# Weights of seven experts split ahead of time by GpSimd, and their halves loaded from scratch memory

## The reference

```python
x = x + L0_ffn(L0_cond(x, itok_B_1_198, ...), ...)
x = x + L1_ffn(L1_cond(x, itok_B_0_7, ..., fside_8xS_0), ...)
# cond: w = weights[index[b]]; out = einsum('bct,bcd->bdt', x, w) (+ bias[b] in layer 1)
# layer 0 ffn: 8 experts of rank 8 (LoRA) on a shared 512 -> 2048 -> 512 with gelu, top 2
#   h = gelu(x W1' + b1 + 2 z1 B1), y = h W2' + b2 + 2 z2 B2, res += w_topk[k] * y
# layer 1 ffn: top 2 of 8 experts, hidden width 352, and a shared expert, hidden width 704
g = silu(einsum('td,edh->teh', x, w_gate)) * einsum('td,edh->teh', x, w_up)
routed = einsum('teh,ehd,te->td', g, w_down, comb)
shared = silu(x @ sw_gate) * (x @ sw_up) @ sw_down
out = routed + shared
```

## Time and profile before

| | |
|---|---|
| median of 3 runs | 1048.93 us |
| the profiled execution, own time | 1050.06 us |
| its span | 1048.2 us |
| TensorE busy | 1010.6 us (96%) |
| VectorE, ScalarE, GpSimd busy | 50%, 30%, 34% |
| mean granted TensorE clock | 0.993 |
| DMA over the span | 136.41 MB, 130 GB/s |

### The profile page before, as it was taken

One profiled execution on the slowest core, in us unless ns is written; L12 is line 12 of the kernel. 1 busy time (PEld: TensorE's weight loads), 2 busy tenths in 40 slices (PEclk: granted clock), 3 DMA queues, 4 the chain that ended last, 5 costly groups with the idle time before them and its releaser, 6 DMA issues.

```text
span 1048.2 us, 14852 instructions
## 1 busy us (share of the span) xinstructions
PE 1010.6 (96%) x4893; PEld 837.2 (80%) x4895; DVE 524.3 (50%) x886; ACT 314.4 (30%) x550; POOL 354.5 (34%) x351
## 2 busy tenths in 40 slices
PE   8899999999999999999999999999989999999993
PEld 5678887888888887888867777778778999999992
DVE  3788777455565455555566333665543314443000
ACT  3743332211121112111242010301144545454541
POOL 4123245410000000000042000022168889898873
PEclk9999999999999999999999999999999999999997
DMA  7387543443433434453444101005155665665433
GB/s 239 130 297 272 161 136 122 166 161 114 140 123 121 153 128 161 142 181 123 138 159 151 41 1 41 1 1 198 58 187 108 163 163 142 141 146 119 80 61 40
DMA packets 51322, 136.41 MB, mean 130 GB/s; under 512 B 8708, under 2 KB 10004, under 8 KB 50772
## 3 DMA queue, kind: packets, MB, share of 16 engines
q1 hardware_dynamic: 36660, 108.15, 30.1%
q0 software_dynamic: 12432, 25.71, 12.4%
q10 hardware_dynamic: 2192, 2.08, 0.7%
HBM read 96.85 MB, written 39.07 MB: 130 GB/s over the span
## 4 chain that ended last, share of the span: by engine, by line
PE 85%; DVE 4%; POOL 4%; DMA 2%; issue 1%; ACT 1%; ACTq 1%; PEldq 0%; POOLq 0%; PEld 0%; DVEq 0%
PE ps_y L1687 6%; PE ps_y L1689 6%; PE ps_y L1688 5%; PE ps_h L1645 5%; PE ps_h L1647 5%; PE ps_h L1646 5%; PE ps_u L1700 3%; PE ps_u L1699 3%; PE ps_h L1933 2%; PE ps_y L1933 2%; PE ps_y L1928 2%; PE ps_y L1929 2%; PE ps_y L1856 2%; PE ps_y L1857 2%; PE ps_h L1840 2%; PE ps_h L1841 2%
## 5 line engine op out<-in xcount | busy, mean ns | idle before, releaser
L1202 DVE TENSOR_TENSOR h<-h,wb 128x512 f32<-128x512 f32 x64 | 44.4, 693 | 162.6 <-ACT h L903 162.5
L897 ACT ACTIVATE h<-ps_h,bias 128x512 f32<-128x512 f32 x64 | 44.0, 689 | 235.1 <-PE ps_h L1654 235.1
L685 POOL DMA_DIRECT2D s_raw<-in_sgu x8 | 4.3, 544 | 299.9 <-DVE g_lo L1210 192.1
L1687 PE MATMUL ps_y<-w_hi,g_hi 128*128 (+1 forms) x256 | 102.2, 399 | 3.5 <-DVE g_lo L1210 3.5
L1689 PE MATMUL ps_y<-w_hi,g_lo 128*128 (+1 forms) x256 | 101.2, 395 | 0.0
L1688 PE MATMUL ps_y<-w_lo,g_hi 128*128 (+1 forms) x256 | 101.0, 395 | 0.0
L1645 PE MATMUL ps_h<-xt_hi,w_hl 128*128 128x512 f32 x256 | 100.0, 391 | 0.7 <-ACT lg_t L846 0.7
L1647 PE MATMUL ps_h<-xt_hi,w_hl 128*128 128x512 f32 x256 | 100.3, 392 | 0.0
L1646 PE MATMUL ps_h<-xt_lo,w_hl 128*128 128x512 f32 x256 | 100.2, 391 | 0.0
L1477 DVE CAST eg_hi<-e_raw 128x704 fp32r<-128x704 f32 x32 | 16.7, 581 | 138.0 <-PE ps_y L1958 125.3
L903 ACT ACTIVATE h<-ps_h,bias 128x512 f32<-128x512 f32 x64 | 43.9, 688 | 115.4 <-PE ps_h L1667 115.4
(11 more groups left out here) (319 smaller groups left out, 2455.5 us busy)
## 6 DMA issues: line engine op xcount, KB each, us to landing
w_hl<-w1s_d SPq DMA_DIRECT2D x49, 704.0 KB, 4.1
w1s_d<-w_hl SPq DMA_DIRECT2D x16, 704.0 KB, 5.9
e_raw<-in_wgu SPq DMA_DIRECT2D x8, 1408.0 KB, 7.1
w_raw<-in_w1b SPq DMA_DIRECT2D x16, 608.0 KB, 4.7
xres<-in_x SPq DMA_DIRECT2D x16, 256.0 KB, 4.5
acc<-x_d SPq DMA_DIRECT2D x4, 1024.0 KB, 7.6
xc_d<-xc SPq DMA_DIRECT2D x4, 1024.0 KB, 4.8
e_raw<-in_wdn SPq DMA_DIRECT2D x8, 512.0 KB, 8.4
```

Of the source, the lines that this page charges most:

```text
L1202: tt(h1[u][:], h1[u][:], wb[:, v, :], ALU.mult).then_inc(gch, 1)
L1687: mm(ps_y[:, j, :], g_hi[u][:, cols], sl(w2_hi), start=first, **kw)
```

## The change

The raw weights of experts 1 to 7 are laid out by the host as `we1`, (7, 128, 4608): per partition gate and up (2816 numbers), down (1536), and padding. GpSimd splits them in layer 0, from the end of the first super tile on, in 42 units of 128 x 768 (six for an expert): it loads a unit, casts it to `pre_hi`, stores that to scratch memory `e_d`, subtracts in place and stores the low half. The raw units go through two buffers for the first units and then three, two of which lie in `u1t`; the high halves through two. Unit k is loaded at the earliest when step 16 + (k - 2) is over. VectorE's first shared split, GpSimd's own and SyncE's first load of halves wait until all units are stored, since their destinations share memory with the units' buffers or they read them. Expert 0 stays as it was.

In the routed stage SyncE loads the four finished pieces of an expert straight into the buffers that TensorE reads (`load_halves`, 11264 and 6144 bytes a partition) and then counts the expert as done. VectorE makes xg_lo, rg and rgt_lo, reading PSUM itself, so that ScalarE's copies xg_f, ru and rgt_f are gone; xg_hi and xg_lo have two buffers. TensorE turns x of tile t+2 before up of tile t+1, and x of tile 0 within the last shared super tile. Tiles 0 and 1 are gathered without waiting for the last shared gate. GpSimd keeps the gathers and scatters; tile t is scattered right after its own gather step. A matrix of layer 1's conditioning and its bias column are one load, two for each w1 split, between the splits.

```diff
+    UNITS, UW = 6, we1.shape[2] // 6
+    AHEAD = UNITS * (E - 1)
+    IN_TWO = 8
+    raw_of = [k % 2 if k < IN_TWO else (k - IN_TWO) % 3 for k in range(AHEAD)]
+    raw_used = [raw_of[:k].count(raw_of[k]) for k in range(AHEAD)]
+    e_d = scr("e_d", (E - 1, 2, P, UNITS * UW))
...
+        pre_hi = [sb_ahead(f"pre_hi{u}", [P, UW], F32R)[:] for u in range(2)]
+        pre_raw = [sb_ahead("pre_raw0", [P, UW])[:], u1t[:, 0:UW], u1t[:, UW:2 * UW]]
...
-            for s in range(NS):
+            def load_halves(e):
+                b, gu = e % 2, DC * 2 * H1
+                for k, (eg, ed) in enumerate(((eg_hi, ed_hi), (eg_lo, ed_lo))):
+                    sp.dma_start(eg[:, b].rearrange("p c n -> p (c n)").bitcast(F32),
+                                 e_d[e - 1, k, :, 0:gu]).then_inc(half_in, 16)
+                    sp.dma_start(ed[:, b].rearrange("p c n -> p (c n)").bitcast(F32),
+                                 e_d[e - 1, k, :, gu:gu + HC * D]).then_inc(half_in, 16)
+            for s in range(NS - 1):
                 store_acc(s)
+            for u in range(2):
+                sp.wait_ge(pre_hi_st[u], 16 * (AHEAD // 2))
+            for u in range(3):
+                sp.wait_ge(pre_lo_st[u], 16 * raw_of.count(u))
+            sp.wait_ge(gu_done, NS * SH)
+            load_halves(1)
+            store_acc(NS - 1)
             for e in range(1, E):
-                load_expert(e)
+                if e >= 2:
+                    tiles = sp.value_load(last_tile[0:1, e:e + 1], min_val=0, max_val=SLOT_TILES)
+                    sp.wait_ge(ry_done, 1 + tiles)
+                    load_halves(e)
+                sp.wait_ge(half_in, 64 * e)
+                sp.wait_ge(e_done, e)
+                sp.sem_inc(e_done, 1)
...
+            def load_unit(k):
+                u = raw_of[k]
+                pool.wait_ge(d_done, 2 + FT + max(k - 2, 0))
+                if u == 2 and not raw_used[k]:
+                    pool.wait_ge(z_ok, 6)
+                if raw_used[k]:
+                    pool.wait_ge(pre_lo_st[u], 16 * raw_used[k])
+                at = k % UNITS * UW
+                pool.dma_start(pre_raw[u], we1[k // UNITS, :, at:at + UW]).then_inc(pre_in[u], 16)
+            def high_unit(k):
+                u = k % 2
+                pool.wait_ge(pre_in[raw_of[k]], 16 * (raw_used[k] + 1))
+                if k >= 2:
+                    pool.wait_ge(pre_hi_st[u], 16 * (k // 2))
+                nc.gpsimd.tensor_copy(pre_hi[u], pre_raw[raw_of[k]]).then_inc(pre_hi_done, 1)
+                pool.wait_ge(pre_hi_done, k + 1)
+                at = k % UNITS * UW
+                pool.dma_start(e_d[k // UNITS, 0, :, at:at + UW], pre_hi[u].bitcast(F32)).then_inc(pre_hi_st[u], 16)
+            def low_unit(k):
+                raw = pre_raw[raw_of[k]]
+                nc.gpsimd.tensor_tensor(raw.bitcast(F32R), raw, pre_hi[k % 2].bitcast(F32), ALU.subtract)\
+                    .then_inc(pre_lo_done, 1)
+                pool.wait_ge(pre_lo_done, k + 1)
+                at = k % UNITS * UW
+                pool.dma_start(e_d[k // UNITS, 1, :, at:at + UW], raw).then_inc(pre_lo_st[raw_of[k]], 16)
+            def units(ks):
+                for k in ks:
+                    high_unit(k)
+                    if k <= IN_TWO:
+                        load_unit(k + 1)
+                    if IN_TWO <= k < AHEAD - 2:
+                        load_unit(k + 2)
+                    low_unit(k)
+            shared_at = (NS - 2) * FT + 2
+            load_unit(0)
+            units(range(shared_at))
...
+            units(range(shared_at, AHEAD))
...
             for t in range(SLOT_TILES):
-                g_low(t)
-                if t + 1 < SLOT_TILES:
-                    products(t + 1)
-                if t + 2 < SLOT_TILES:
-                    x_low(t + 2)
                 if t + 5 < SLOT_TILES:
                     gather(t + 5)
-                if t:
-                    scatter_add(t - 1)
-            scatter_add(SLOT_TILES - 1)
+                scatter_add(t)
...
-            def x_high(t, first=False):
+            def x_high(t, u):
                 act.wait_ge(xgt_done, t + 1)
-                nc.scalar.copy(xg_hi[:].rearrange("p c n -> p (c n)"), ps_u[:, 0, :]).then_inc(xg_hi_done, 1)
-                if not first:
-                    act.wait_ge(xg_lo_done, t)
-                nc.scalar.copy(xg_f[:], ps_u[:, 0, :]).then_inc(xg_f_done, 1)
+                nc.scalar.copy(xg_hi[u][:].rearrange("p c n -> p (c n)"), ps_u[:, 0, :]).then_inc(xg_hi_done, 1)
...
+                else:
+                    for u in range(2):
+                        dve.wait_ge(pre_hi_st[u], 16 * (AHEAD // 2))
+                    for u in range(3):
+                        dve.wait_ge(pre_lo_st[u], 16 * raw_of.count(u))
...
-            for e in range(1, E):
-                dve.wait_ge(e_in, 48 * (e + 1))
-                if e >= 2:
-                    tiles = dve.value_load(last_tile[0:1, e:e + 1], min_val=0, max_val=SLOT_TILES)
-                    dve.wait_ge(ry_done, 1 + tiles)
-                for k in range(4):
-                    split_expert(e, e % 2, k)
+            def x_low(t, u):
+                dve.wait_ge(xg_hi_done, t + 1)
+                tt(xg_lo[u][:].rearrange("p c n -> p (c n)"), ps_u[:, 0, :],
+                   xg_hi[u][:].rearrange("p c n -> p (c n)").bitcast(F32), ALU.subtract).then_inc(xg_lo_done, 1)
+            def products(t, u, first=False):
+                dve.wait_ge(rs_done, t + 1)
+                dve.wait_ge(rup_done, t + 1)
+                if not first:
+                    dve.wait_ge(rgt_done, t)
+                tt(rg[:, 0:H1], rs[:], ps_y[:, u, 0:H1], ALU.mult).then_inc(rg_done, 1)
+            def g_low(t):
+                dve.wait_ge(rgt_hi_done, t + 1)
+                tt(rgt_lo[:].rearrange("p c n -> p (c n)"), ps_u[:, 1, 0:HC * P],
+                   rgt_hi[:].rearrange("p c n -> p (c n)").bitcast(F32), ALU.subtract).then_inc(rgt_lo_done, 1)
+            def slot_tile(t, u, nxt=True, nxt2=True):
+                g_low(t)
+                if nxt2:
+                    x_low(t + 2, u)
+                if nxt:
+                    products(t + 1, 1 - u)
...
+                    if (s, j) == (NS - 1, 0):
+                        turn_x(0, 0, 16, first=True)
...
                     gate_or_up(t + 1, 1 - u, after, 0)
                 turn_g(t)
+                if nxt2:
+                    turn_x(t + 2, x_buf, n)
                 if nxt:
                     gate_or_up(t + 1, 1 - u, after, 1)
```

More of the change, by code:

```diff
@@ L339, in adaln_ffn @@
         out_st = sem("out_st")
+        pre_in = [sem(f"pre_in{u}") for u in range(3)]
+        pre_hi_done = sem("pre_hi_done")
+        pre_lo_done = sem("pre_lo_done")
+        pre_hi_st = [sem(f"pre_hi_st{u}") for u in range(2)]
+        pre_lo_st = [sem(f"pre_lo_st{u}") for u in range(3)]
+        half_in = sem("half_in")
         e_in = sem("e_in")
@@ L442, in load_block, with load_matrix @@
                           cond0[bass.ds(b * SEQ, SEQ), :]).then_inc(landed, 16)
[L444 to L453, removed]
+        def load_matrix(eng, j, h):
+            at = j * 2 + h
+            b = eng.value_load(it_row[1][0:1, at:at + 1], min_val=0, max_val=cond1.shape[0] // SEQ - 1)
+            eng.dma_start(cw1[h * SEQ:(h + 1) * SEQ, j, :], cond1[bass.ds(b * SEQ, SEQ), :]).then_inc(cw1_in[h], 16)
         @block.sync
@@ L1036, in copies @@
                     silu(t + 1, 1 - u)
-                g_high(t, first=stored is None and n == 0)
-                if nxt:
-                    up(t + 1, 1 - u)
+                g_high(t)
                 if nxt2:
-                    x_high(t + 2)
+                    x_high(t + 2, u)
                 weigh(t, n, stored)
-            x_high(0, first=True)
+            x_high(0, 0)
             silu(0, 0, first=True)
-            up(0, 0)
-            x_high(1)
+            x_high(1, 1)
             act.wait_ge(sy_done, NS * TPS)
@@ L1544, in _ @@
                             split_expert(0, 0, k)
[L1547 to L1553 removed]
+            def x_low(t, u):
[18 more added lines that the diff above has]
+                    products(t + 1, 1 - u)
+            x_low(0, 0)
+            x_low(1, 1)
+            products(0, 0, first=True)
+            for t in range(2):
+                slot_tile(t, t)
+            with dve.Fori(1, (SLOT_TILES - 2) // 2) as m:
+                for u in range(2):
+                    slot_tile(m * 2 + u, u)
+            for t in range((SLOT_TILES - 2) // 2 * 2, SLOT_TILES):
+                slot_tile(t, t % 2, t + 1 < SLOT_TILES, t + 2 < SLOT_TILES)
         @block.tensor
@@ L1869, in slot_sums, with turn_x @@
                 last.then_inc(oh_mm, 1)
+            def turn_x(t, u, n, first=False):
+                pe.wait_ge(xg_in[u], n)
+                if not first:
+                    pe.wait_ge(xg_lo_done, t)
+                for c in range(DC):
```

(10 more changed lines are left out.)

99 lines of the change are left out of this document (39 added, 60 removed).

## The result

The changed kernel takes 1076.82 us (median of 4 runs, 1074.62 to 1080.04), the kernel before beside it 1049.45 us (4 runs): a ratio of 1.0259, 95% interval 1.0237 to 1.0281. It is slower by 27 us; 1039.0 was forecast, and the range ended at 1053.

What follows compares the result with a forecast made beforehand. TensorE's in-order queue was taken as the bound. Terms of -5.3, -5.7, -4.4 and +5.5 us sum to -9.9, from 1048.93 to 1039.0 us; range 1031.5 to 1053 us.

Steps and rivals of the forecast that it cites:

- Layer 0, VectorE: GpSimd's unit arithmetic holds up VectorE's chain before g_lo in layer 0: 0 to 0.5 us a unit, taken as +5.5 us.
- the second rival: In layer 0, GpSimd's copy and subtraction make TensorE wait for g_lo: 0.6 us a unit, 25 us, 1058 us; chance 0.10.
- The opening: At the start of the routed stage, reordered turns and earlier gathers remove TensorE waits: -5.3 us.
- The rest of the routed stage: Over the later routed tiles, 5.7 of the 6.2 us that TensorE loses to waits are taken back.
- The end: After the last weighings, scatters no longer queue behind the next tile's GpSimd operations: -4.4 us.
- The fourth rival: In the routed stage, double bytes make experts late and scatters lag, so only the opening is earned: 1049 us; chance 0.06.
- The transfers in layer 0: 1.15 MB more per step in layer 0 still lets w_hl's reload land in time: no cost, 0.8 us from one.
- GpSimd in time: GpSimd finishes all 42 units before VectorE's first shared split, at a period of 7.7 us: no cost.
- the third rival: GpSimd's unit period in layer 0 exceeds 8.0 us, so VectorE's first shared split waits: 1044 to 1056 us; chance 0.12.

Runs made afterwards that it cites:

- the gap and the chain: Changed kernel, complete, with each unit's rounding and subtraction started after VectorE's last operation of a step: 1051.01 us; started at ScalarE's second gelu instead: 1064.13 us.
- the first experiment: Changed kernel without GpSimd's arithmetic on the units, except two roundings; all loads, stores and landing waits stay: 1037.48 us, ratio 0.9872.

## Why the prediction was wrong

**The step that failed** is "Layer 0, VectorE", put at 0.13 us for each of 42 units, 5.5 us in all, with an upper bound of 0.5. It was 1.0 us, 42.1 in all, which is what the second rival says, and more than its 0.6. Two things in it were wrong.

The phase. I wrote that at 7.7 against 7.4 us it drifts and about every third unit falls on the chain. 35 of 42 did. A drift needs two clocks, and there weren't two: the subtractions are 8.54 us apart (42 from 173.97 to 523.95) and the steps in that time 8.57. It is not the hold that ties them together. With the rounding alone the steps are back at 7.39 us and the units with them (the roundings start at 385.86, 393.24 and 400.67), and with the moves alone the units are 7.38 us apart. In all three kernels most loads of a unit wait for the landing of a low half (27 of 42 in the changed kernel, 37 with the moves alone), so the units follow a cycle of transfers that runs beside SyncE's one reload a step; whether that ties them is not shown. Nor is why they keep to the chain when the subtraction is there (31 of 42 start in it or within 0.3 us before it) and to the time behind it when only the rounding is. What the gap and the chain show is that the place decides, at the same work. With the phase held in the chain on purpose a unit cost 0.74 us.

The length. I counted one hold against the spare 1.5 us, of "up to its own length". In the bad phase the subtraction and the next unit's rounding follow each other within 0.9 us (330.47 to 331.33), each catches another operation of the same chain, and their holds add: 2.95 us. The bound of 0.5 a unit, about 2.1 less 1.5, left out the second hold and was no bound; the lengths themselves were put too high (1.86 and 0.84 us measured, up to 2.1 each forecast). The evidence I leaned on, that 16 splits before cost only 3 waits, had one long GpSimd subtraction a step, issued at one place.

**What was right.** The opening: 5.3 forecast, 5.9 measured from the end of the shared stage; the forecast had the 0.5 us of tile 0's turn in it, so 5.4 by its own counting. The rest of the routed stage: 5.7 against 7.8, since all 6.2 us of waits went and the cadence fell from 6.745 to 6.70 us, 1.6 us in 36 tiles: the two tiles that I had read as free of waits took 6.69 and 6.79, and now every tile takes 6.70. The end: 4.4 against 3.3; from tile 37's weighing to the end (1058.85; 1028.37 before) it is 16.5 instead of 19.8 us, less than forecast because the scatters did lag: that of tile 37 starts 1.8 us behind its weighing, not 0.3. The chain that ended last is nearly all one scatter behind the other from 953 us on, and the first two of these are the long ones:

```profile
958.90 9.93 DMA out_x<-yt,slot_tok
...
993.12 9.57 DMA out_x<-yt,slot_tok
...
1061.33 4.49 DMA out_x<-yt,slot_tok
```

Their 9.9 and 9.6 us, twice the usual 4.5 to 5, fall into loads of an expert's halves. SyncE issues six such loads in the routed stage (at 838, 865, 905, 932, 959 and 992 us), and within 4 us of each starts one scatter that takes 9.6 to 10.7 us, while none of the other 33 takes more than 6.6. That points at the loads; no run here takes them away. The fourth rival's lag is thus real, but it cost some 1.1 us of what was forecast for the end and nothing in the stage before it.

The transfers in layer 0: about 1 us, by the first experiment, where nothing was forecast. GpSimd in time: yes, VectorE's first shared split starts at 557.03, long after the last unit, though its period was 8.5 us and not 7.7; the third rival's limit of 8.0 was for steps of 7.4, and the steps were longer. Where they were 7.39, with the rounding alone, the period was 7.4 too.

Sum of the measured terms: 42.1 + 2.1 (the part of the 44.2 that lies behind layer 0, of which the turn of tile 0 is 0.5) - 5.9 - 7.8 - 3.3 = +27.2 us; the difference of the two spans is 27.1.

## What to carry to other kernels

When GpSimd gets arithmetic beside a VectorE chain that TensorE waits for, add up all GpSimd operations that can fall in one chain, and compare the sum, not one of them, with what is to spare; count on the bad phase unless a semaphore excludes it: two streams of nearly the same period did not drift past each other here, with the arithmetic or without. Before giving GpSimd an operation for free, look at what VectorE would take for it in its own idle stretch: here 0.95 us in a gap of 3.7 did what 1.85 us on GpSimd could not do at any place that was tried. And look for the few long waits: one of 6.2 us cost 9.1, because the clock was lower behind it.
